# Attention row maxima reduced over two PSUM banks at once, in a ring of two bank pairs

## The reference

```python
q = _w8a8_linear(_layernorm(x), wq, bq)        # (B, H, N, D)
k, v = cond @ wk.T + bk, cond @ wv.T + bv      # (B, H, L, D)
scores = jnp.einsum('bhnd,bhld->bhnl', q, k) * inv_sqrt_d + mask[:, None]
attn = jax.nn.softmax(scores, axis=-1)
x = x + _w8a8_linear(jnp.einsum('bhnl,bhld->bhnd', attn, v), wo, bo)
gate, up = silu(_qlinear(ln(x), wq_gate, s_gate)), _qlinear(ln(x), wq_up, s_up)
x = x + _qlinear(gate * up, wq_down, s_down)
```

## Time and profile before

| | |
|---|---|
| median of three runs | 547.08 us (543.87 to 549.44) |
| the profiled execution's own time | 546.88 us |
| its span in the profile | 545.1 us |
| PE busy | 490.1 us, 90% |
| DVE busy | 400.2 us, 73% |
| ACT busy | 257.4 us, 47% |
| POOL busy | 247.0 us, 45% |
| first score of group 0 | 146.51 us |
| last score of group 7 | 397.65 us |

### The profile page before, as it was taken

One profiled execution on the slowest core, in us unless ns is written; L12 is line 12 of the kernel. 1 busy time (PEld: TensorE's weight loads), 2 busy tenths in 40 slices (PEclk: granted clock), 3 DMA queues, 4 the chain that ended last, 5 costly groups with the idle time before them and its releaser, 6 DMA issues.

```text
span 545.1 us, 7041 instructions
## 1 busy us (share of the span) xinstructions
PE 490.1 (90%) x2372; PEld 310.1 (57%) x2377; DVE 400.2 (73%) x616; ACT 257.4 (47%) x460; POOL 247.0 (45%) x132
## 2 busy tenths in 40 slices
PE   4999688989899999999999769998879999889994
PEld 3887466677454454444444334433348877768883
DVE  2889861898867878787779887868787577465454
ACT  3539732421365656565656635569544314312220
POOL 3005700703076778787887728767341111112120
PEclk9999898899889999999999979999899999899998
DMA  7897898498393909173553700012033433254522
GB/s 234 292 348 265 319 313 249 163 261 276 93 241 126 185 1 189 26 147 67 113 101 65 149 1 2 1 43 74 2 116 96 156 117 117 95 180 150 159 73 77
DMA packets 44389, 77.41 MB, mean 142 GB/s; under 512 B 5280, under 2 KB 13504, under 8 KB 44352
## 3 DMA queue, kind: packets, MB, share of 16 engines
q1 hardware_dynamic: 44352, 76.94, 48.7%
HBM read 57.95 MB, written 18.87 MB: 141 GB/s over the span
## 4 chain that ended last, share of the span: by engine, by line
PE 60%; DVE 23%; DMA 7%; issue 5%; ACT 3%; SPq 1%; POOLq 0%; POOL 0%; DVEq 0%; ACTq 0%
PE ps L740 12%; PE ps L789 10%; PE ps L769 9%; PE ps L880 6%; PE ps L881 6%; DVE pmax L1258 3%; PE ps L899 3%; PE ps L900 3%; PE ps L691 2%; DMA raw<-in_ctx_t 2%; DVE p_sum L1402 2%; DMA raw<-in_wk_t 2%; DVE kq_lo L1231 2%; DVE c_lo L1158 2%; PE ps L701 2%
## 5 line engine op out<-in xcount | busy, mean ns | idle before, releaser
L1258 DVE TENSOR_REDUCE pmax<-ps 128x1 f32<-128x512 f32 x256 | 162.4, 684 | 39.3 <-PE ps L740 38.7
L1040 ACT ACTIVATE p_t<-ps 128x512 f32<-128x512 f32 x256 | 133.1, 600 | 78.5 <-PE ps L769 74.4
L740 PE MATMUL ps<-k_st,q_st 96*128 96x512 f32 x256 | 106.7, 444 | 12.7 <-DVE pmax L1258 11.0
L1561 POOL TENSOR_TENSOR p_sum<-p_sum,p_t 128x1024 f32<-128x1024 f32 x46 | 110.2, 2407 | 5.1 <-ACT p_t L1040 2.6
L1561 POOL TENSOR_TENSOR p_sum<-p_t 128x1024 f32<-128x1024 f32 x30 | 70.9, 2382 | 77.5 <-PE ps L691 63.2
L769 PE MATMUL ps<-q_st,k_st 97*128 97x512 f32 x256 | 98.5, 432 | 4.8 <-ACT p_t L1040 4.7
L740 PEld LDWEIGHTS ps<-k_st,q_st 96*128 96x128 f32 x256 | 46.7, 194 | 82.5 <-DVE pmax L1258 47.0
L1570 POOL TENSOR_TENSOR q_st<-v_gr,k_st 128x512 fp32r<-128x512 f32 x22 | 28.2, 1284 | 106.6 <-ACT k_st L1131 106.6
L880 PE MATMUL ps<-xt_hi,k_st 128*128 128x512 f32 x176 | 70.4, 400 | 1.4 <-DVE xt_lo L1363 1.4
L789 PE MATMUL ps<-p_t,v_gr 128*32 128x512 f32 x512 | 69.5, 615 | 0.8 <-ACT p_t L1040 0.7
L881 PE MATMUL ps<-xt_lo,k_st 128*128 128x512 f32 x176 | 69.5, 395 | 0.0
(11 more groups left out here) (117 smaller groups left out, 649.4 us busy)
## 6 DMA issues: line engine op xcount, KB each, us to landing
k_st<-k_hi_d SPq DMA_DIRECT2D x16, 512.0 KB, 6.8
mask_sb<-in_mask SPq DMA_DIRECT2D x3, 2048.0 KB, 11.2
w_int<-in_w_gate SPq DMA_DIRECT2D x22, 256.0 KB, 2.7
w_int<-in_w_up SPq DMA_DIRECT2D x22, 256.0 KB, 3.0
w_int<-in_w_down SPq DMA_DIRECT2D x22, 256.0 KB, 3.5
raw<-in_ctx_t SPq DMA_DIRECT2D x16, 256.0 KB, 6.1
k_hi_d<-kq_hi SPq DMA_DIRECT2D x16, 256.0 KB, 5.4
k_lo_d<-kq_lo SPq DMA_DIRECT2D x16, 256.0 KB, 6.2
```

Source lines behind the costliest of these rows:

```text
L740: mm = pe.matmul(dst, q_st[g % SLOTS][0:3 * D, j, P * nt:P * nt + P], k_st[g % SLOTS][0:3 * D, j, 512 * lh:512 * lh + 512], start=True, st ...
L1040: act.activation(p_t[:, q % 4, j, :], ps[:, score_bank(lc, j), :], ACT.Exp).then_inc(exp_done, 1)
L1258: dve.tensor_reduce(pmax[:, g % 2, u:u + 1], ps[:, ring_bank(("M", g, u)), :], AX_X, ALU.max).then_inc(max_read, 1)
L1561: pool.tensor_tensor(p_sum[:, half, :, :], former, p_t[:, q % 4, hs, :], ALU.add).then_inc(added_pool, 1)
```

## The change

- A unit is now 128 queries against all 1024 keys: two matmuls into two neighbouring banks, and one DVE reduction over both (axes XY), which writes the negated maximum straight into neg_m. `shift`, pmax and the semaphore m_parts go. There are 16 units in a group, two in a step; 6 run ahead.
- The ring has two pairs of banks (0 and 1, 2 and 3) instead of three banks; an entry waits for the entry two before it. TO and TS share one entry, and tail pieces go in twos: O 0 and 1 in group 5 step 5, and so on.
- The scores have two banks (4 and 5) instead of three. A step's order is S0, U, S1, U, S2, PV, S3, and then sums, R, turn and tail.
- Sums are made in steps 2 and 6, the turn in step 4 (before: 3). p_sum has two totals in turn, so an addition waits for the sums two before.
- The later projections go round four banks (4 to 7) instead of five.
- A scratch for dynamic transfers is set to 2048 bytes, which makes room for p_sum.

```diff
-                key, bank = (kind, n, j), (3 + (turn + 2) % 5 if bank0 is None else bank0 + j)
+                key, bank = (kind, n, j), (4 + turn % 4 if bank0 is None else bank0 + j)
...
-        UNITS = HG * NT * 2
+        UNITS = HG * NT
...
-        AHEAD = 12
-        SHIFT_LC, ROWS_LC = (UNITS - AHEAD) // HG - 1, (UNITS - AHEAD) // HG
-        TURN_LC = 3
+        AHEAD = 6
+        PER_STEP = UNITS // LC
+        ROWS_LC = (UNITS - AHEAD) // PER_STEP
+        TURN_LC = 4
...
-            return 3 + (HG * lc + j) % 3
+            return 4 + (HG * lc + j) % 2
...
-                    if r >= 3:
-                        for sem_value in ring_emptied(RING[r - 3]):
+                    if r >= 2:
+                        for sem_value in ring_emptied(RING[r - 2]):
...
-                        if at >= 3:
-                            pe.wait_ge(exp_done, HG * LC * g + at - 2)
+                        if at >= 2:
+                            pe.wait_ge(exp_done, HG * LC * g + at - 1)
                         elif g >= 1:
                             pe.wait_ge(exp_done, HG * LC * g)
...
-                    dve.tensor_reduce(pmax[:, g % 2, u:u + 1], ps[:, ring_bank(("M", g, u)), :], AX_X, ALU.max).then_inc(max_read, 1)
+                    dve.tensor_reduce(neg_m[:, g % 2, nt, j:j + 1], ps[:, bank:bank + 2, :], AX_XY, ALU.max,
+                                      negate=True).then_inc(max_read, 1)
...
-                    dve.wait_ge(sum_done, q // SET)
+                    dve.wait_ge(sum_done, q // SET - 1)
...
-                    elif q > SET:
-
-                        pool.wait_ge(sum_done, q // SET)
+                    elif q > 2 * SET:
+
+                        pool.wait_ge(sum_done, q // SET - 1)
```

More of the change, by code:

```diff
@@ L13 @@
 AX_X = mybir.AxisListType.X
+AX_XY = mybir.AxisListType.XY
 LN_EPS = 1e-5
@@ L335, in ring_of_step @@
         def ring_of_step(g, lc):
-            ahead = [divmod(UNITS * (g + 1) + AHEAD + HG * lc + i, UNITS) for i in range(HG)]
+            ahead = [divmod(UNITS * (g + 1) + AHEAD + PER_STEP * lc + i, UNITS) for i in range(PER_STEP)]
             units = [("M", of, u) for of, u in ahead if of < G]
             rows = [("R", g + 1)] if lc == ROWS_LC and g + 1 < G else []
-            turned = [("TO", g - 1), ("TS", g - 1)] if lc == TURN_LC and g >= 1 else []
-            return units, rows, turned, [("tail", *key) for key in TAIL_AT.get((g, lc), [])]
+            turned = [("T", g - 1)] if lc == TURN_LC and g >= 1 else []
+            return units, rows, turned, [("tail", *TAIL_AT[g, lc])] if (g, lc) in TAIL_AT else []
         RING = [("M", 0, u) for u in range(UNITS)]
@@ L362, in ring_emptied @@
             if kind == "tail":
-                return [tail_emptied(0, *key[1:])]
+                return [tail_emptied(0, key[1], key[2] + k) for k in range(2)]
             return [(o_done, g + 1)]
@@ L690, in sums @@
                 for j in range(HG):
-                    mm = pe.matmul(ps[D * j:D * j + D, SUM_BANK, :], ones[:, :], p_sum[:, j // 2, j % 2, :],
+                    mm = pe.matmul(ps[D * j:D * j + D, SUM_BANK, :], ones[:, :], p_sum[:, i % 2, j // 2, j % 2, :],
                                    start=(i % per_group == 0), stop=(i % per_group == per_group - 1))
@@ L1106, in _ @@
                     for key in ring_of_step(g, lc)[-1]:
-                        tail_part(0, *key[1:], ring_bank(key))
+                        for k, bank in enumerate(ring_banks(key)):
+                            tail_part(0, key[1], key[2] + k, bank)
                     if lc == ROWS_LC and g + 1 < G:
```

111 lines of the change are left out of this document (51 added, 60 removed).

## The result

| | before | changed |
|---|---|---|
| median, same chip | 545.48 us (542.98 to 549.44, 4 runs) | 565.50 us (558.62 to 568.79, 4 runs) |
| ratio | | 1.032, 95% interval 1.019 to 1.045 |
| span of the profiled execution | 545.1 us | 567.0 us |

The changed kernel is 3.2% slower.

A forecast was written before the change was run, and what follows sets the result against it. PE was taken to bound the kernel, DVE mattering where PE waits. Terms: start +3.7, group 0 +1.5, groups 1 to 3 3 x 1.6, then +2.3, -1.8, +3.8, +1.5, sum +15.8 on 546.9: 563 us, range 549 to 574.

The forecast's parts named there:

- A better ring can give little: Middle groups: only some 1.9 us of waits for DVE per group can be given back; plain steps gain nothing.
- The score bank's turn: Score, exponential, next score takes 1.19 us against 1.045 available; with copy and group change, 1.97 us lost a group.
- 31.5 us for a middle group: Middle group's length from first score to first score: 31.5 us, 1.6 more than 29.90.
- Reductions of 1.22 alone, 1.13 in a row: DVE's two-bank reduction, in us; saves about 9 us of DVE busy time, worth nearly 0 on the path.
- Group 5: -1.8: Group 5 shortens from 40.96 to 39.2 us; DVE's operation still waits behind POOL's adds, PE waits about 2.2 us.
- Group 6: +3.8: Group 6 grows from 31.20 to 35.0 us: a shared-entry unit 1.3 us late, then steps paced by two score banks.
- Start: +3.7: Before the first score: two projection tiles meet taken banks, 4.1 and 3.3 us late; +3.7 us, bounds 0 and 5.5.
- The second p_sum buffer: POOL no longer waits for the sums, but nothing is gained in the middle groups.
- Group 7: Held by DVE's chain up to its middle, the same in both kernels; its last steps lose 1.5 us.
- (a): Rival: no change, 549 us, because a score's turn fits under 1.045 us in a running step; chance 0.13.
- (b): Rival: faster, 536 us, because PE's 11.0 us of idle time before units goes and nothing replaces it; chance 0.08.
- (c): Rival: slower still, 572 us, by group 5's operation missing POOL's pause, 1.4 us reductions, clock falling at the start; chance 0.13.

The follow-up runs named there:

- a_order2: Changed kernel with the second unit of a step cut in two around the second score; 568.79 us, ratio 1.048 to the kernel before.
- a_bound: Changed kernel with a group's first scores waiting only for the exponential that read their own bank; 559.95 us, ratio 1.029 to the kernel before.
- the last mend: ACT's output copy put ahead of step 0's fourth exponential, added in a_best to the edits of a_order2 and a_bound; together 553.80 us.
- a_no_sqrt: Changed kernel with ACT's square root in group 7 replaced by a plain copy, without its two table loads; 559.05 us, ratio 1.024.
- a_k2: Changed kernel with the projections' round of four banks begun one bank later; 565.81 us.
- a_best_no_sqrt: Changed kernel with the edits of a_best and a_no_sqrt together; 551.68 us, ratio 1.012 to the kernel before.
- b_two_scores2: Kernel before with two score banks and a step order made for them, its ring of three single banks kept; 571.16 us, ratio 1.052.
- a_best: Changed kernel with three mends: a_order2's order, a_bound's waits, ACT's output copy before step 0's fourth exponential; 553.80 us, ratio 1.020.

## Why the prediction was right, and where it was not

The forecast was 563.0 us, in a range of 549 to 574; the median came at 565.5. Point by point:

- **A better ring can give little.** Right. PE's idle time before units that DVE ended fell from 11.0 to 3.2 us, and the group got longer. With the score turns mended the pairs gave about 0.3 us a group.
- **The score bank's turn, 1.19 us, lost 0.25 us in three steps, 0.27 by the copy and 0.95 at the change of group: 1.97.** The mechanism is shown part by part: S1 stands 1.19 behind S3; a_order2 took 0.43 out of the group, a_bound 0.74, and the last mend 0.63 more where 0.24 was expected. Together 1.80 (31.25 to 29.45). The late S1 and the copy were one wait in step 1: a_order2 left that step at 3.59 us, and all three mends brought it to 3.18.
- **31.5 us for a middle group.** Measured 31.25. The waits behind the turn, put at 0.40 for U1 of step 5 and 0.43 for U0 of step 6, are there: 0.30 and 0.44 by distance.
- **Reductions of 1.22 alone, 1.13 in a row.** 1.217 on the mean. DVE's busy time fell by 20 us, not by 9: the reductions alone by 11.7 (162.4 to 150.7), and 4.1 more because group 7's normalization (6.04 us before, 1.92 now) no longer ran beside POOL's adds. It wasn't what counted.
- **Groups 0 and 4: +1.5 and +2.3.** Measured +2.5 (+1.6 in a_no_sqrt, whose group 0 has the same code) and +1.8.
- **Group 5: -1.8.** Measured -1.6, in good part by luck. The forecast had the first rounding wait behind POOL's adds from 11.1 to 16.6 us of the group, and named an operation under 2 us as a sign of being wrong. It came at 11.1 and took 0.84; the second one behind it took 2.75, and PE's longest wait was 1.60 us where 2.2 was forecast:

```profile
318.78 0.84 DVE L1203 TENSOR_SCALAR o_sb<-o_sb 128x1024 f32<-128x1024 f32 x1
319.65 2.75 DVE L1204 TENSOR_SCALAR mask_sb<-o_sb 128x1024 bf16<-128x1024 f32 x1
```

  So that sign came, and the walk through this meeting was wrong. Step 3 takes 3.16 us (12.97 before), and the other seven steps together 8.2 more. Kernels with the same code in this group took 36.9 and 41.0 us (with four banks for projections, and the kernel before), and those like the changed one 38.0 to 39.6.
- **Group 6: +3.8.** Measured +3.9. The steps fit: step 4 takes 1.6 us more (5.55 against 3.98; 1.3 was forecast) and steps 5 to 7 together 2.0 more. But no experiment took group 6 apart; it stays argued.
- **Start: +3.7.** Both waits came as predicted (K 2's first tile 3.82, K 3's first 2.47), and the profile shows +3.4. But a_k2 took the first wait away and the start stayed, and kernels with equal code differ by 2.8 us. The waits are real and the price was wrong: the forecast added both waits, and by a_k2 what K 2's tile loses is made up before K 3's. On the mean over kernels the start moved by 0.9 us.
- **The second p_sum buffer: worth nothing.** Wrong. The forecast looked at POOL's load in the middle groups, and not at what else the adds' time changes. It is worth 0.25 us in each of groups 1 to 3 and 3.7 us in group 7, and the kernel before with that part alone is faster by 0.6% (0.2 to 1.0).
- **Group 7: "held by DVE's chain up to its middle, the same in both; its last steps lose 1.5".** This is the term that was mis-sized: it measured +9.5 in the profile and 5.9 in three kernels with the same code. DVE held it before (PE's 2.69 us in step 4), but not now: DVE waits 6 us for ACT's square root there. ACT's table loads stop the exponentials for 2.8 us. Three score banks had covered that but for 0.54 us; two don't, and the low clock behind the pause adds 2.3 us to the 2.85 of that step. Since the changed kernel has the two totals too, the loss may be set against 25.5 and not 29.2: some 9.6 us of loss with 3.7 of gain in it, and both were missed.

The start's term was too large by some 2.8 and group 7's too small by 4.4 (by the like kernels). That they partly cancel, and that group 5 came out near by another way, is luck, and so the total is nearer than the terms. What the forecast had right by its mechanism is the score bank's turn in the middle groups. Of the rivals, (a) and (b) fell with the turn of 1.19 us, which both needed to be shorter. (c) had a falling clock as one of its causes, at the start; it fell in group 7.

What stays open: how much of group 7's remaining 5 us (30.6 in a_best_no_sqrt, 25.5 with three score banks and two totals) is the turn of the score banks alone; group 6's 3.1 us, which no experiment took apart; and the price of the start, for which the profiles of single executions spread too far.

## What to carry to other kernels

Banks are one stock: before giving one engine's ring a fourth bank, measure the turn of what loses one (here score, exponential, next score: 1.19 us) against the time the order leaves it, and look for the longest pause of the engine that empties it: here the plain step lost 0.25 us to the missing bank, and ACT's one pause of 2.8 us lost 5 us in one step. When a change has parts, run each alone: here the one that was thought worthless was a gain, and hid part of the loss of the others. A wait that is removed in front of another one, as K 2's in front of K 3's, moves and doesn't pay; compare the end of the stage over several kernels with equal code before believing a difference of 3 us.

## What the runs showed of the hardware

- **What the lower clock followed.** In the changed kernel PE stood for 2.93 us, and the clock was at 0.50 for 17.1 us from within that pause on; in the kernel before it stood for 2.69 us, and 3.4 us at 0.50 followed; in b_two_scores2 it stood for 2.45 us and the clock stayed at 1.00; in a_no_sqrt the clock fell (0.66 in a window of 5 us) though PE never stood longer than 1.1 us in group 7. So one pause's length doesn't tell. How long it lasts varies too: behind the same pause of 2.93 us it was 17.1 us in the changed kernel, 6.8 in a_k2, a_bound and a_order2, and 3.4 in a_best. In a_k2 it was back at 1.00 before 400 us:

```profile
395.00:400.00 5.00, 4.67 (x20) 1.34 (x20) 1.51 (x2) 2.44 (x5) 2.36 (x1) 0.62 0.00 0
400.00:405.00 5.00, 4.54 (x29) 1.92 (x22) 0.00 (x0) 3.21 (x6) 2.38 (x1) 1.00 0.01 3
```

- **The spread of one kernel goes with the mean granted clock.** The four runs of the changed kernel: 558.62 us at 0.972, 564.32 at 0.963, 566.67 at 0.954, 568.79 at 0.948.
- **A table load takes 1.28 us, and changing the function and back takes two** (389.42 and 390.93). The Trainium skill, "ScalarE: Activation LUTs" (section "What ACT_TABLE_LOAD costs"), gives 1283 ns for one, and the trace agrees. It adds some 1380 ns of drain for each switch, and its section "Table sets: the hidden batching unit" puts exp and then sqrt at two loads, about 5.3 us; the trace shows no such drain, since the last exponential ends at 389.40 and the square root starts at 390.71, and load, square root and load take 2.8 us together. ACT was 48% busy over the span, and the price was PE's pause and PE's clock.
- **The same DVE instruction takes 0.68 us or 5.57**, as it meets POOL's adds: 5.57 in the earlier trace rows, 3.78, 2.82 and 0.94 in the kernels above for the rounding L1201, 0.68 where POOL pauses. Group 5, with no change to its own code, moved between 36.9 and 41.0 us, with the clock at 0.50 for 6.8 us in both.
